# Seven block products instead of eight for one feature chunk of a LoRA feed-forward kernel

## The reference

```
gate = x Wg' + 0.5 (x Ag') Bg'          # Ag, Bg, ...: one of 16 adapters per sequence, rank 16
up   = x Wu' + 0.5 (x Au') Bu'          # 1376 features
act  = silu(gate) * up
down = act Wd' + 0.5 (act Ad') Bd'      # 512 features
x    = x + down sign(W0)' + bias0
x    = x + (x B1' A1') Weff' + bias1    # one of 64 adapters per sequence, rank 16
```

## Time and profile before

| | us |
|---|---|
| median of 3 runs (893.67 to 895.75) | 893.84 |
| the profiled execution, own time | 894.13 |
| its span, first to last instruction | 892.3 |
| PE busy | 886.9 (99%) |
| DVE busy | 411.4 (46%) |
| ACT busy | 203.7 (23%) |
| POOL busy | 122.4 (14%) |

### The profile page before, as it was taken

The page is one execution under the profiler, slowest core; times in us unless marked ns, Lnnn a source line. Parts: engine busy times, 40 slices in busy tenths (PEclk is TensorE's granted clock), DMA queues, the critical chain, the costliest instruction groups (busy, mean ns, idle before and its releaser), DMA issues.

```text
span 892.3 us, 22052 instructions
## 1 busy us (share of the span) xinstructions
PE 886.9 (99%) x7564; PEld 731.0 (82%) x7564; DVE 411.4 (46%) x986; ACT 203.7 (23%) x381; POOL 122.4 (14%) x141
## 2 busy tenths in 40 slices
PE   9999999999999999999999999999999999999998
PEld 6888888888888888888888888888888888888886
DVE  5854444444344544435354453444444344444444
ACT  4852212112121221212122221121222212122120
POOL 0200111011111111011111001111101111110111
PEclk9999999999999999999999999999999999999999
DMA  9934464554555555555555555555555455555553
GB/s 346 418 114 131 130 167 125 152 145 133 161 135 154 134 150 149 130 160 142 153 129 150 150 141 145 151 143 138 148 152 143 136 157 138 154 136 149 148 128 91
DMA packets 148947, 137.33 MB, mean 154 GB/s; under 512 B 54848, under 2 KB 120384, under 8 KB 148800
## 3 DMA queue, kind: packets, MB, share of 16 engines
q1 hardware_dynamic: 91744, 111.11, 43.2%
q10 hardware_dynamic: 56240, 22.83, 9.9%
q0 software_dynamic: 944, 3.15, 0.9%
HBM read 94.80 MB, written 11.01 MB: 119 GB/s over the span
## 4 chain that ended last, share of the span: by engine, by line
PE 98%; DVE 1%; DMA 0%; ACT 0%; issue 0%; SPq 0%; DVEq 0%
PE gu_ps L859 57%; PE y_ps L896 27%; PE out_ps L918 3%; PE gu_ps L1004 3%; PE out_ps L969 2%; PE gu_ps L995 1%; PE out_ps L905 1%; PE y_ps L859 1%; PE out_ps L859 1%; PE gu_ps L896 1%; PE out_ps L926 1%; DMA lb_raw<-in_lbw 0%; DVE a_lo L645 0%; PE gu_ps L1033 0%; DVE weff_raw L791 0%; PE y_ps L973 0%
## 5 line engine op out<-in xcount | busy, mean ns | idle before, releaser
L859 PE MATMUL gu_ps<-wu_sb,xT_sb 128*128 128x432 f32 (+1 forms) x1152 | 261.3, 371 | 0.0
L859 PE MATMUL gu_ps<-wg_sb,xT_sb 128*128 128x432 f32 (+1 forms) x1152 | 254.5, 370 | 0.5 <-DVE act_all L663 0.5
L896 PE MATMUL y_ps<-down_sb,actT_sb 128*128 128x512 f32 x1023 | 241.5, 393 | 0.0
L896 PEld LDWEIGHTS y_ps<-down_sb,actT_sb 128*128 128x128 f32 x1023 | 189.6, 188 | 60.2 <-issue 21.4
L859 PEld LDWEIGHTS gu_ps<-wg_sb,xT_sb 128*128 128x128 f32 x1152 | 216.3, 188 | 25.9 <-DVE xT_sb L645 1.4
L859 PEld LDWEIGHTS gu_ps<-wu_sb,xT_sb 128*128 128x128 f32 x1152 | 214.1, 188 | 21.4
L645 DVE TENSOR_TENSOR actT_sb<-landed,actT_sb 128x512 fp32r<-128x512 f32 (+1 forms) x96 | 60.9, 635 | 191.9 <-ACT actT_sb L480 191.8
L480 ACT CAST actT_sb<-landed 128x512 fp32r<-128x512 f32 (+1 forms) x96 | 56.1, 585 | 309.4 <-DMA landed<-act_all 194.0
L439 POOL TENSOR_TENSOR x_in<-x_in,bias_sb 128x512 f32<-128x512 f32 x32 | 41.2, 1287 | 615.9 <-DMA x_in<-in_x 615.9
L645 DVE TENSOR_TENSOR xT_sb<-xT_raw,xT_sb 128x512 fp32r<-128x512 f32 x32 | 22.1, 692 | 105.3 <-ACT xT_sb L480 105.3
L677 DVE TENSOR_TENSOR t_own<-out_ps,const_sb 128x64 f32<-128x64 f32 x32 | 7.2, 225 | 135.5 <-PE out_ps L918 133.0
(11 more groups left out here) (128 smaller groups left out, 557.5 us busy)
## 6 DMA issues: line engine op xcount, KB each, us to landing
b_rows<-in_btab SPq DMA_DIRECT2D x128, 236.0 KB, 3.1
a_raw<-in_atab SPq DMA_DIRECT2D x128, 152.0 KB, 2.3
landed<-act_all SPq DMA_DIRECT2D x132, 64.0 KB, 2.1
xT_raw<-in_xT SPq DMA_DIRECT2D x32, 256.0 KB, 2.6
x_in<-in_x SPq DMA_DIRECT2D x32, 256.0 KB, 2.8
landed<-act_all ACTq DMA_DIRECT2D x124, 64.0 KB, 2.2
out_x<-out_sb SPq DMA_DIRECT2D x31, 256.0 KB, 2.9
x_landed<-x_turn ACTq DMA_DIRECT2D x122, 64.0 KB, 2.2
```

The source lines that it names most:

```text
L859: last = nc.tensor.matmul(o, w, m, start=start and n == 0, stop=stop and n == len(terms) - 1, skip_group_check=not check)
L896: last = nc.tensor.matmul(to[:], actT_sb[:, ACTT_SLOT[c] + n, a, :], down_sb[:, blk, b, :], start=begin and (c, n) == (0, 0) and (a, b) == ...
```

## The change

```diff
-            def up(g, c, pieces=range(KC)):
-                f, w = CHUNKS[c]
-                if 0 in pieces and first(g):
-                    pe.wait_ge(S["wu_lo"], 2 * KC if c == 1 else NC * KC)
...
+            def mid(bank, x_parts, w, signal, start):
+                product(gu_ps[bank][:], [(x_parts(k, a), w[:, b, k, :]) for k in range(HALF) for a, b in THREE], signal,
+                        start=start, check=False)
+            def p3(g, j):
...
+                pe.wait_ge(L["mid_sum"], nth(MID_SUM, "u4", j))
+                pe.wait_ge(L["s_lo"], nth(S_SPLIT, "s4", j))
+                mid(1, s_of(0), w22_sb, L["mid_mm"], False)
+            def p4(g, j):
+                pe.wait_ge(L["mid_sum"], nth(MID_SUM, "up_odd", j))
+                slot_ready(g, 1, 4, 2 * j)
+                mid(0, x_of(1), slot_sb[1], L["mid_mm"], False)
...
-            def step(g, prev, pp):
+            def step(g, j, parity, prev, pp):
                 gate(g, 0)
-                if not first(g):
+                if parity == 0:
+                    p1(g, j)
+                    p6(g, j)
+                    p5(g, j)
                     up(g, 0)
-                gate(g, 1)
-                up(g, 1, range(0, 1))
-                small_ready(g, prev, pp)
-                up(g, 1, range(1, 2))
-                small(prev, pp)
-                up(g, 1, range(2, 4))
-                if first(g):
+                    p2(g, j)
+                    p3(g, j)
+                    small_ready(g, prev, pp)
+                    small(parity, prev, pp)
+                    pe.wait_ge(L["mid_sum"], nth(MID_SUM, "u2", j))
+                else:
+                    p7(g, j)
                     up(g, 0)
+                    p4(g, j)
+                    small_ready(g, prev, pp)
+                    small(parity, prev, pp)
...
+            def odd_products(g, j):                                       # DVE
+                dve.wait_ge(L["mid_mm"], nth(MID_MM, "p7", j))
+                dve.wait_ge(L["mid_sum"], nth(MID_SUM, "u4", j))
+                nc.vector.tensor_tensor(gu_ps[1][:], u4_sb[:], gu_ps[0][:], ALU.add).then_inc(L["mid_sum"], 1)
+                dve.wait_ge(L["mid_mm"], nth(MID_MM, "p4", j))
+                nc.vector.tensor_tensor(gu_ps[0][:], u2_sb[:], gu_ps[0][:], ALU.add).then_inc(L["mid_sum"], 1)
...
             def step(g, j, parity, prev, pp, nxt):                        # DVE
+                if parity == 0:
+                    even_products(g, j)
+                else:
+                    odd_products(g, j)
                 turn_t(g)
...
+                if parity == 1 and nxt is not None:
+                    first_sums(j + 1)
                 split_actT(g, 0)
                 if prev is not None:
                     add_y(prev)
                     turn_x1(prev)
                 split_actT(g, 1)
+                if parity == 1 and nxt is not None:
+                    low_s(1, j + 1)
+                    low_s(2, j + 1)
                 split_actT(g, 2)
...
+                if parity == 1 and nxt is not None:                       # ACT, behind copy_lhs
...
+                    load_t(1, L["slot0_in"], L["mid_mm"], nth(MID_MM, "p7", j))
+                    load_t(2, L["slot1_in"], L["mid_mm"], nth(MID_MM, "p4", j))
...
+                if n == 4:                                                # DVE, start of the program
+                    first_sums(0)
+                if n == 5:
+                    dve.wait_ge(S["t_raw"], nth(T_RAW, "t2"))
+                    low_t(1, t1_raw)
...
-            def add_bias0(g):
-                pool.wait_ge(L["x_in"], 16 * g + 16)
-                nc.gpsimd.tensor_tensor(x_in[:], x_in[:], bias_sb[:, 0, :], ALU.add).then_inc(L["x_biased"], 1)
```

More of the change, by code:

```diff
@@ L40 @@
 PAIR = CHUNKS[0][1] + CHUNKS[1][1]
-ROW = 3 * 512
+MID_MM = ("p1", "p6", "p5", "p3", "p7", "p4")
+MID_SUM = ("u2", "u4", "up_even", "up_odd", "gate_odd")
+S_RAW = ("s1", "s2", "s3", "s4_part", "s4")
+S_SPLIT = ("s1", "s2", "s4", "s3")
+T_RAW = ("t1", "t3", "t2", "t4")
+MID_SPLIT = ("w11", "w21", "w22")
+MID = CHUNKS[1][1]
+SIDE = CHUNKS[2][1] + CHUNKS[0][1]
+SIDE_AT = {2: 0, 0: CHUNKS[2][1]}
+SIDE_ROW = 7 * P
+HALF = KC // 2
+FOLDED_FIRST = 7
 LINE = 512
@@ L850, in _ @@
-            step(G - 1, G - 2, G - 3, None)
+            split_mid("w21", w21_sb, w21_raw, "t4")
+            split_mid("w22", w22_sb, w22_raw, "t2", "t3")
+            for r in range(4):
+                nc.vector.tensor_copy(act_all[group(r), F:FP], ident[group(r), group(r)]).then_inc(S["pad_set"], 1)
+            dve.wait_ge(S["pad_set"], 4)
+            step(0, 0, 0, None, None, 1)
+            step(1, 0, 1, 0, None, 2)
+            step(2, 1, 0, 1, 0, 3)
+            step(3, 1, 1, 2, 1, 4)
@@ L851, in _ @@
+            with dve.Fori(2, G // 2 - 1) as j:
+                step(2 * j, j, 0, 2 * j - 1, 2 * j - 2, 2 * j + 1)
+                step(2 * j + 1, j, 1, 2 * j, 2 * j - 1, 2 * j + 2)
+            step(G - 2, G // 2 - 1, 0, G - 3, G - 4, G - 1)
+            step(G - 1, G // 2 - 1, 1, G - 2, G - 3, None)
             finish(G - 1)
@@ L878, in up, with side @@
-            def up(g, c, pieces=range(KC)):
-                f, w = CHUNKS[c]
-                if 0 in pieces and first(g):
-                    pe.wait_ge(S["wu_lo"], 2 * KC if c == 1 else NC * KC)
-                last = product(gu_ps[GU_BANK[c][1]][:, 0:w], [(xT_sb[:, k, a, :], wu_sb[:, b, k, f:f + w])
-                                                              for k in pieces for a, b in THREE], None,
-                               start=0 in pieces, stop=KC - 1 in pieces)
-                if c == NC - 1 and KC - 1 in pieces:
-                    last.then_inc(L["xT_used"], 1)
+            def side(x_at, w, w_at):
+                return [(x_at[:, k, a, :], w[:, b, k, w_at]) for k in range(KC) for a, b in THREE]
@@ new lines, in gate, with up @@
+            def gate(g, c):
+                w = CHUNKS[c][1]
+                if c == 0:
+                    if first(g):
+                        pe.wait_ge(S["wg_lo"], KC)
+                    pe.wait_ge(L["xT_lo"], g + 1)
+                if not first(g):
+                    pe.wait_ge(L["act_done"], g * NC - NC + c + 1)
+                product(gu_ps[GU_BANK[c][0]][:, 0:w], side(xT_sb, wg_sb, slice(SIDE_AT[c], SIDE_AT[c] + w)), None)
+            def up(g, c):
+                w = CHUNKS[c][1]
+                if c == 0 and first(g):
+                    pe.wait_ge(S["wu_lo"], KC)
+                product(gu_ps[GU_BANK[c][1]][:, 0:w], side(xT_sb, wu_sb, slice(SIDE_AT[c], SIDE_AT[c] + w)),
+                        L["xT_used"] if c == 2 else None)
@@ new lines, in p5, with p2 @@
+            def p5(g, j):
+                pe.wait_ge(L["s_lo"], nth(S_SPLIT, "s1", j))
+                slot_ready(g, 0, 1, 2 * j - 1)
+                mid(1, s_of(0), slot_sb[0], L["mid_mm"], True)
+            def p2(g, j):
+                if first(g):
+                    pe.wait_ge(S["wmid_lo"], nth(MID_SPLIT, "w21"))
+                pe.wait_ge(L["p1_out"], j + 1)
+                mid(0, x_of(1), w21_sb, None, False)
+            def p3(g, j):
+                if first(g):
+                    pe.wait_ge(S["wmid_lo"], nth(MID_SPLIT, "w22"))
+                pe.wait_ge(L["mid_sum"], nth(MID_SUM, "u4", j))
+                pe.wait_ge(L["s_lo"], nth(S_SPLIT, "s4", j))
+                mid(1, s_of(0), w22_sb, L["mid_mm"], False)
@@ L960, in small_ready, with small @@
                     after(pe, L["out_done"], pp)
-            def small(prev, pp):
-                last = t_rows()
+            def small(parity, prev, pp):
+                last = t_rows(parity)
                 if prev is not None:
```

475 lines of the change are left out of this document (335 added, 140 removed).

## The result

The changed kernel takes 955.03 us (median of 6 runs, 947.43 to 961.95) against 893.86 before. The ratio is 1.067, 95% interval 1.064 to 1.070. One of the six runs, 961.95, was in a slower state and is left out of the ratio; the other five have a median of 953.61. The forecast was 889.6 with a range of 878 to 899: wrong in sign and by 65.

The account below looks back on a forecast made before the run. PE, busy 99% of the span, was taken as the bound: 894.13 - 22.2 for removed matmuls + 10.0 + 4.2 + 3.8 for waits = 889.9, or 889.6 in terms of the median; range 878 to 899.

Parts of the forecast that it names:

- PE's work removed, 22.2: Gate and up products: 16 pairs lose 6 matmuls of 512 columns each, 96 at 0.231, saving 22.2 us.
- p4's wait in odd steps, 10.0: Fifteen odd steps, 3 to 31: p4 waits for DVE to read P7, starting at 6.64 instead of 6.05; +10.0 us.
- Step 1, 4.2: Step 1: p4, due at 6.1 after gate 0, starts at 10.2 because up odd ends at 10.1; +4.2 us.
- p6 needs S2's low part ... 0.2 spare: Even steps: PE could start p6 at 3.5 after gate 0, due at 3.73, so no wait was counted.
- the slower rival: Loop: T loads ahead of ACT's activation tiles make p6 late, giving 917, or 898 with 0.8 late; with thin chains 0.16.
- In by 21.6: Slower rival, odd steps: T1 and T2 take 7.7 at 272 GB/s and land by 21.6, or 24.6 if descriptors bind.
- The rival's 1.8 for the quarters: Slower rival: chunk 1's activation tile about 2 late, p6 1.8 late in 15 steps, 27 us in all.
- The clock, 2.3 to 3.5 behind the pause of step 1: Rival: PE's clock falls to 1.2 GHz behind step 1's pause, costing 2.3 to 3.5, so 892 to 893; chance 0.12.
- The start, 3.8: Step 0: p3 starts at 69.5 instead of 65.7, waiting for S4 behind DVE's work; +3.8 us.
- PE's order up to 55.49: Start of the program: PE's order up to 55.49 was taken to stay as before.
- POOL's sums, costed at nothing: Start: POOL's four T sums of 1024 columns end by 53, when DVE asks for the last, costing nothing.
- x of group 1, which I had as the hold-up: Start: x of group 1 lands at about 50.3, holding DVE; if in time, 1.4 of the 3.8 remains.

Follow-up runs that it names:

- S early: Edit to the changed kernel: S1 and S2 are split ahead of actT by ACT and DVE; alone 925.82 us, ratio 1.031 to 1.038.
- the run with T early: Changed kernel with ACT issuing the loads of T1 and T2 before move_ad instead of behind copy_lhs: 950.64 us, ratio 1.060 to 1.064.
- the three reorderings: S1 and S2 split ahead of actT, small ahead of p4, step 1's gate 2 early; on the changed kernel without the loop's T loads: 887.52 us, 0.990 to 0.995.
- 893.9: Changed kernel plus the three reorderings, T loaded at half the bytes and split again, POOL's bias addition behind actT's last split, T2's split behind Silu: 893.90 us, ratio 1.0002.
- the next: The 893.9 kernel with DVE adding y to x and turning it ahead of its split of actT's chunk 0: 895.25 against 895.21 us.

## Why the prediction was wrong

- **PE's work removed, 22.2: right.** 96 matmuls are gone, and with T out of the way and S early even steps last 27.3, forecast 27.2.
- **p4's wait in odd steps, 10.0: right.** The sum of DVE ends it, 15 times. p4 starts at 6.89 in the mean, forecast 6.64.
- **Step 1, 4.2: right.** Timeline of PE in the kernel after: p4 starts 10.18 after gate 0, forecast 10.2. The same rows show p3 of step 0 late, and both behind their pauses at half clock: 6 matmuls take 2.64 and 2.93, not 1.6.

```profile
71.34 2.64 PE L1093 MATMUL gu_ps<-w_sb,s_sb 128*128 128x512 f32 x6 [2.25 <-DVE s_sb L785]
...
81.98 2.56 PE L1093 MATMUL gu_ps<-wg_sb,xT_sb 128*128 128x432 f32 x12 [0.52 <-DVE act_all L803]
...
92.16 2.93 PE L1093 MATMUL gu_ps<-slot,xT_sb 128*128 128x512 f32 x6 [3.88 <-DVE gu_ps L910]
```

- **"p6 needs S2's low part ... 0.2 spare", taken as 0: this step failed.** p6 was 2.37 late in the mean: 2.37 x 15 = 35.6. Two inputs were wrong. DVE's split of chunk 1 was taken to end 2.46 after gate 0, as before, though 2 MB were put in front of the quarters it waits for; it ended at 4.23, 1.8 later. The two low parts behind it were priced alone, 0.84, though POOL's addition stands beside them; they took 1.74, 0.9 more. The second input was wrong even without T: p6 was 0.8 late there. Behind the pauses came a cost that the step didn't have, the half clock: p6 and p5 take 3.65 in the mean, forecast 2.77, which is 0.88 x 15 = 13. And a miss was sized at "0 to 4.5", though the case of late T, written down as the slower rival with 917 or 898, had a chance of 0.16.
- **"In by 21.6", at the 272 GB/s left over: right by a sum that isn't shown.** The rival's own terms give 11.9 + 7.7 = 19.6 (and 22.6 for 24.6); 2.0 is added without a word. Measured, T was in at 21.6 of the odd step. But the DMA engines were full (1.03) until the end of `down`, and what was asked for in that time landed late. The rival's 1.8 for the quarters is what they cost; it lacked POOL's part and the clock.
- **Where the 60.7 went:** even steps 30.58 against 27.2 (50.7 over 15), odd ones 24.08 against 23.77 (4.7 over 15), and step 2 begins 4.7 later (110.7 against 99.4 - 1.4 for the first pair's matmuls + 3.8 + 4.2 = 106.0). That is 60.1; 0.6 is not placed.
- **The clock, 2.3 to 3.5 behind the pause of step 1: right as a mechanism, and it was left out of the sum.** It fell where the rival named it, in steps 0 and 1, and also in the loop, behind p6's pauses, in 8 of 15 pairs. Stretches of 71.34 and of 92.16, the last three numbers PEclk, DMA share and GB/s:

```profile
71.34:74.00 2.66, 2.66 (x12) 1.67 (x16) 2.17 (x3) 1.59 (x2) 0.46 (x1) 0.56 0.00 0
92.16:94.90 2.74, 2.74 (x6) 1.81 (x6) 0.00 (x0) 0.00 (x0) 0.00 (x0) 0.50 0.61 192
```

- **The start, 3.8: short by 4.7 up to step 2.** p3 of step 0 started at 71.34, forecast 69.5: 1.8. From there to step 1 it took 10.64, against 9.16 in the run with T early, where the clock stayed full behind the same pause of 2.25: 1.5. Step 1 took 28.76, forecast 27.4: 1.4, all of it behind p4 at half clock. Two readings of the start were wrong: PE's order up to 55.49 did not stay (gate 0 began at 58.72), and POOL's sums, costed at nothing, stretched what DVE did beside them by about 5; putting them on DVE costs the same. x of group 1, which I had as the hold-up, was in time.
- **Without the T loads** the order of the change gives 913.0, not 889.6: p6 0.8 late and the start account for most of it. Only with the three reorderings as well is it 887.5. That the forecast lies near this is luck: the 10.0 for p4's wait is in the forecast and not in this order of work.

What stays open: the last 6 us between 893.9 and 887.5, odd steps of 23.90 against 23.34. In one run they are waits for x, in the next for rows; which transfer delays them wasn't told apart.

## What to carry to other kernels

A load that has 20 us to land is not free: ask what is asked for while it is under way, on any queue, and how much spare time each of those has. Place big transfers where no small one on the path is in flight, or halve them. Price a DVE instruction with what POOL does beside it. A spare time of 0.2 in a chain with DMA, ACT, DVE and POOL in it is none; and behind pauses of PE of 2.1 to 3.3 another 1.3 to 1.6 went in clock, in 8 of 12 cases.

## What the runs showed of the hardware

- DVE instructions with two SBUF operands beside a POOL `tensor_tensor`: 1.22 to 2.78 for 1024 columns, 0.68 to 1.70 for 512, 0.42 to 2.01 for a sum of 256, and 0.42 to 1.5 for a low part of 256 in the loop. One with a PSUM operand stayed at 0.67. The Trainium skill (SBUF — State Buffer, "Who interferes with whom") has the two engines share a port pair under a lock; the runs agree and give the sizes, in both directions: POOL's addition of bias1 takes 1.63 in the mean here (1.66 in the kernel before, also beside DVE) and 1.29 in the 893.9 kernel, where it was moved behind DVE's splits.
- Small transfers on one queue beside 1 MB on another: the last of the quarters of 64 KB took 7.0 from issue to landing in the mean with T1 asked for by SP beside them, and 2.6 with T1 asked for behind them.
- Behind 12 pauses of 2.1 to 3.3 before p6, the next 12 matmuls took 4.1 to 4.5 in 8 cases (the granted clock at its lower level, 1.2 GHz, for most of them) and 2.8 to 2.9 in 4. With ten matmuls put in the pause it was 2.7 to 2.9 always. A pause of 2.2 to 2.6 before p3 of step 0, in all 19 traces of changed kernels, was followed by a lower clock in 14 and by the full one in 5.
